# Delta-rule layer: last value product and diagonal transposes moved up, key squares in one instruction, value load ahead of the output load

## What is computed

```python
x = x + _L0_attn_ref(_layernorm(x), ...)        # softmax attention
x = x + _L0_ffn_ref(_layernorm(x), ...)         # 48 experts
x = x + _L1_attn_ref(_layernorm(x), ...)        # the delta rule, below
x = x + _L1_ffn_ref(_layernorm(x), ...)         # 16 experts

# _L1_attn_ref, per head, chunks of 64 tokens
qkv = silu(_causal_conv1d(qkv, conv_weight))    # 4 taps
q, k = _l2norm(q) * Dk ** -0.5, _l2norm(k)
attn = -((k_beta @ k.T) * decay_mask), strictly lower; then a row-by-row solve -> (I - attn)^-1
value_corrected, k_cumdecay = attn @ v_beta, attn @ (k_beta * g_exp)
for c in chunks:
    v_prime = v_c - kcd_c @ state
    out = (q_c @ state) * ge_c + intra @ v_prime
    state = state * gel_c + (k_c * kd_c).T @ v_prime
core = _rmsnorm(core * silu(z), norm_weight); out = core @ W_out
```

## Time and profile before

| | us |
|---|---|
| median of 3 runs | 1714.47 (1711.51 to 1717.37) |
| profiled execution | 1714.89 |
| its span | 1713.2 |
| delta rule, first to last start of a body (15 bodies) | 584.9 to 1533.4 |
| a full body, mean of the 13 from 645.5 to 1476.3 | 63.9 |

### The profile page before, as it was taken

How to read it: one execution, slowest core, us unless ns; L and a number is a source line. 1 busy time by engine, 2 the same in 40 slices (tenths; PEclk the granted TensorE clock), 3 DMA queues, 4 the chain that set the end, 5 groups by cost and what they waited for, 6 DMA issues and landing times. The chain is left out here.

```text
span 1713.2 us, 38604 instructions
## 1 busy us (share of the span) xinstructions
PE 1428.9 (83%) x14345; PEld 1025.2 (60%) x14345; DVE 1139.4 (67%) x2334; ACT 856.3 (50%) x2403; POOL 780.6 (46%) x1118
## 2 busy tenths in 40 slices
PE   5888993199555889999999999999999999986665
PEld 2443442166422667767767767767777777775465
DVE  6886127823566778788778777778788878643623
ACT  3334861043043575665665665665665666532122
POOL 5000000277114266456556466556566656553343
PEclk9998996599776999999999999999999999988688
DMA  8100005085813464554555555654555545241783
GB/s 280 66 2 2 2 1 154 7 234 178 254 49 88 107 146 124 147 149 134 139 146 139 128 152 134 139 147 142 133 147 149 137 143 151 76 117 56 223 259 128
DMA packets 249434, 218.72 MB, mean 128 GB/s; under 512 B 88770, under 2 KB 224962, under 8 KB 247200
## 3 DMA queue, kind: packets, MB, share of 16 engines
q1 hardware_dynamic: 234992, 192.41, 41.4%
q0 software_dynamic: 5712, 15.60, 2.8%
q10 hardware_dynamic: 8544, 8.26, 1.5%
HBM read 133.85 MB, written 82.25 MB: 126 GB/s over the span
## 5 line engine op out<-in xcount | busy, mean ns | idle before, releaser
L1544 PE MATMUL d_big<-all_xn_t,all_w 128*128 128x512 f32 x512 | 264.2, 649 | 17.3 <-DVE d_conv L1805 11.4
L1805 DVE SCALAR_TENSOR_TENSOR d_conv<-d_big,all_cw,d_conv 128x1023 f32<-128x1023 f32 (+2 forms) x192 | 245.4, 1278 | 46.4 <-ACT d_conv L2039 43.8
L2277 POOL TENSOR_TENSOR d_y<-d_y,all_xn 128x256 f32<-128x256 f32 x128 | 95.8, 748 | 183.9 <-DVE d_y L1952 153.0
L1544 PEld LDWEIGHTS d_big<-all_xn_t,all_w 128*128 128x128 f32 x512 | 98.2, 207 | 107.8 <-issue 96.7
L2141 ACT COPY d_ys<-d_big 128x128 f32<-128x128 f32 x256 | 60.9, 266 | 198.5 <-PE d_big L1695 139.5
L1733 PE MATMUL d_big<-all_wo,d_yt 128*128 128x256 f32 x512 | 126.5, 393 | 13.6 <-DVE d_yt L1877 13.6
L1666 PE MATMUL d_big<-all_w,all_xn_t 128*128 128x256 f32 x512 | 124.2, 386 | 0.0
L1851 DVE SCALAR_TENSOR_TENSOR d_AI<-d_big,d_b_col,d_decay 128x256 f32<-128x256 f32 x256 | 105.7, 474 | 23.0 <-PE d_big L1557 20.7
L1733 PEld LDWEIGHTS d_big<-all_wo,d_yt 128*128 128x128 f32 x512 | 97.4, 198 | 26.4 <-issue 14.1
L1666 PEld LDWEIGHTS d_big<-all_w,all_xn_t 128*128 128x128 f32 x512 | 93.6, 190 | 18.3 <-issue 7.2
L347 DVE TENSOR_REDUCE a_neg_max<-a_big 128x1 f32<-128x128 f32 (+7 forms) x128 | 90.5, 751 | 13.1 <-PE a_big L276 12.8
(11 more groups left out here) (437 smaller groups left out, 3503.5 us busy)
## 6 DMA issues: line engine op xcount, KB each, us to landing
turned_kq_scratch<-d_turned SPq DMA_DIRECT2D x32, 512.0 KB, 3.9
d_kq_tok<-turned_kq_scratch SPq DMA_DIRECT2D x128, 128.0 KB, 3.1
turned_v_scratch<-d_vs SPq DMA_DIRECT2D x16, 1024.0 KB, 4.1
d_vs<-turned_v_scratch SPq DMA_DIRECT2D x64, 256.0 KB, 5.6
grouped_y_scratch<-d_yx SPq DMA_DIRECT2D x32, 512.0 KB, 3.9
d_yx<-grouped_y_scratch SPq DMA_DIRECT2D x128, 128.0 KB, 3.1
all_w<-in_L_attn_W_qkvz SPq DMA_DIRECT2D x16, 768.0 KB
...
```

The costliest lines, as they stand in the source:

```text
L1544: mm = pe.matmul(big[0][:, c, :], w_sb[par][:, k, n * DK:(n + 1) * DK], xn_t[:, k, c * 512:(c + 1) * 512], start=(k == 0), stop=(k == KD - 1))
L1805: dve.scalar_tensor_tensor(conv[:, sh:T], src[:, 0:T - sh], cw[:, bass.ds(g, 1), COLUMN_OF[j], 3 - sh], conv[:, sh:T], ALU.mult, ALU.add). ...
L2277: pool.tensor_tensor(part, part, zs[:, t, :], ALU.mult).then_inc(s["yg_s"], 1)
```

## The change

1. `iv 7` of the previous group, with its `gather 7`, moves up: on PE from behind `gates 3` to between `l0y 2` and `gates 2`; on DVE from behind tap 1 3 to behind tap 1 1.
2. `l0x` is split into its three transposes; two of them run ahead of tap 1 3, the third behind `l1p`. `kq_turn 1` moves behind these.
3. `ksq` becomes one Square of all keys into the tile `conv`, and a new step `ksum` on DVE (a tensor_reduce over `conv`, ahead of `kb`) sums them. `tap0 2` waits for `ksum`.
4. ACT: `l1p` directly behind `l0y`, then `silu 1`, `gates 3`, `ksq`, `decay`.
5. DVE: `l2p` directly behind `l1y`, products 0 and 1 behind both. PE: products 2 moves from ahead of `l2y` to behind it.
6. SP: `v_in` goes ahead of the previous group's `y_in 0`.

```diff
 SP_ORDER = steps_of("""
-    this solved, v_out; next kq_out 0; prev y_out 0; next kq_in 0; prev y_in 0; this v_in; next kq_out 1, kq_in 1; prev
+    this solved, v_out; next kq_out 0; prev y_out 0; next kq_in 0; this v_in; prev y_in 0; next kq_out 1, kq_in 1; prev
...
-    l0y 2, gates 2, l0y 3, l0y 4, l0y 5, l0y 6, l0y 7, gates 3; prev iv 7; this l1p 0, l1p 1, l1p 2, l1p 3; next proj 2
-    0, proj 2 1; this l1y 0, l1y 1, l1y 2, l1y 3; next products 0; this l2p 0, l2p 1; next products 1, products 2; this
-    l2y 0, l2y 1; next products 3; this y 0, kv 0, iv 0, ks 1; prev out_mm 0 0; this y 1, qs 1, kv 1, iv 1, ks 2, qs 2;
+    l0y 2; prev iv 7; this gates 2, l0y 3, l0y 4, l0y 5, l0y 6, l0y 7, gates 3, l1p 0, l1p 1, l1p 2, l1p 3; next proj 2
+    0, proj 2 1; this l1y 0, l1y 1, l1y 2, l1y 3; next products 0; this l2p 0, l2p 1; next products 1; this l2y 0, l2y 1;
+    next products 2, products 3; this y 0, kv 0, iv 0, ks 1; prev out_mm 0 0; this y 1, qs 1, kv 1, iv 1, ks 2, qs 2;
...
-    this gates 1; prev sq2 4, o1 7; next tap0 1; prev sq2 5; this gates 2, l0y; next silu 1, ksq 0, ksq 1, ksq 2; this
-    l1p; next ksq 3, decay; this gates 3, l1y, l2p; prev sq2 6, sq2 7; this l2y, ys 0; next tap0 2; this ys 1, o1 1;
+    this gates 1; prev sq2 4, o1 7; next tap0 1; prev sq2 5; this gates 2, l0y, l1p; next silu 1; this gates 3; next ksq,
+    decay; this l1y, l2p; prev sq2 6, sq2 7; this l2y, ys 0; next tap0 2; this ys 1, o1 1;
...
+            def ksum(g, par):
+
+                dve.wait_ge(s["ksq_s"], g + 1)
+                dve.tensor_reduce(ss[:, 0, :], conv[:, :].rearrange("p (t n) -> p t n", t=TT), AX.X, ALU.add).then_inc(s["ksum_s"], 1)
...
-            def ksq(g, par, i):
-
-                if i == 0:
-                    act.wait_ge(s["kq_in0"], g * 64 + 64)
-                    if not at(g, 0):
-                        act.wait_ge(s["ek_s"], g)
-                for t in (2 * i, 2 * i + 1):
-                    act.activation(junk[:, :].rearrange("p (q r) -> p q r", r=QB), kq_tok[:, :, t, :], ACT.Square, accum_out=ss[:, 0, t:t + 1]).then_inc(s["sq_s"], 1)
-                    act.wait_ge(s["sq_s"], g * 16 + t + 1)
+            def ksq(g, par):
+
+                act.wait_ge(s["kq_in0"], g * 64 + 64)
+                act.wait_ge(s["silu_s"], g * NJ + 2)
+                act.activation(conv[:, :].rearrange("p (t q r) -> p q t r", q=NQ, r=QB), kq_tok[:, :, 0:TT, :], ACT.Square
+                               ).then_inc(s["ksq_s"], 1)
```

More of the change, by code:

```diff
@@ L1218 @@
     prev state 6; this v_turn 0; prev r 7, gather 5; this v_turn 1; next tap 0 1, tap 0 2, tap 0 3; this qe; next
-    kq_turn 0; prev gather 6; this l0p; next shift, tap 1 1, tap 1 2, tap 1 3; prev gather 7; this l0x; next kq_turn 1;
-    this l1p; prev y_turn 0; next kb; this l1y; next products 0; this l2p; next products 1; this l2y; next products 2;
+    kq_turn 0; prev gather 6; this l0p; next shift, tap 1 1; prev gather 7; next tap 1 2; this l0x 0, l0x 1; next tap 1
+    3; this l1p, l0x 2; next kq_turn 1; prev y_turn 0; next ksum, kb; this l1y, l2p; next products 0, products 1; this l2y; next products 2;
     this state 0, gather 0, r 1; next products 3; this state 1, gather 1; next tap 2 1; this r 2; next tap 2 2; this
@@ L1315, in delta1_phase @@
         names = ("wg_in dt_in a_in ba_mm gate_a gate_v beta_v cum_v clip_v kx_v gx_v ngx_v gam_v cum_rows edge_rows gamma_s col_mm col_a col_v "
-                 "keep_s wide_s masked blank_s eyed made_v const_s rows_in proj_mm tap_s conv_v silu_s kq_x kq_out0 kq_out1 kq_in0 kq_in1 v_x v_out v_in y_x y_out yx_in wo_s sq_s ek_s sv_s bk_s qe_s x_s exp_s edge_s "
+                 "keep_s wide_s masked blank_s eyed made_v const_s rows_in proj_mm tap_s conv_v silu_s kq_x kq_out0 kq_out1 kq_in0 kq_in1 v_x v_out v_in y_x y_out yx_in wo_s sq_s ksq_s ksum_s ek_s sv_s bk_s qe_s x_s exp_s edge_s "
                  "kk_mm ai_s blk_out blk_in sol_v sol_s sol_out y_in vs_s kout_s p0_mm p0_s y0_mm y0_s x0_s p1_mm p1_s "
@@ L1465, in kq_in @@
                 if not at(g, 0):
-                    sp.wait_ge(s["sq_s"], g * 16 - 8 + 8 * a)
+                    if a:
+                        sp.wait_ge(s["sq_s"], g * 8)
+                    else:
+                        sp.wait_ge(s["ksq_s"], g)
                     sp.sem_inc(s["order"], 1)
@@ L1834, in qe_ @@
             def qe_(g, par):
-                dve.wait_ge(s["sq_s"], g * 16 + 16)
+                dve.wait_ge(s["sq_s"], g * 8 + 8)
                 if not at(g, 0) and not at(g, 1):
@@ L1885, in l0p, with l0x @@
                                          ).then_inc(s["p0_s"], 1)
[L1887 to L1893, removed]
+            def l0x(g, par, n):
+                q = (0, 2, 1)[n]
+                own = slice(QB * q, QB * q + QB)
+                half_of = slice(QB * (q % 2), QB * (q % 2) + QB)
+                dve.wait_ge(s["y0_s"], g * 4 + n + 1)
+                dve.transpose(Xc[own, :, half_of], Y[own, :, own]).then_inc(s["x0_s"], 1)
             def l1p(g, par):
@@ L2007, in first @@
                 kq_turn(0, 0, 1)
+                ksum(0, 0)
                 kb(0, 0)
@@ L2022, in first @@
                     tap(0, 0, 3, sh)
-            loop(dve, DVE_ORDER, dict(tap=tap, shift=shift, kb=kb, qe=qe_, products=products, kq_turn=kq_turn, v_turn=v_turn, y_turn=y_turn, l0p=l0p,
+            loop(dve, DVE_ORDER, dict(tap=tap, shift=shift, ksum=ksum, kb=kb, qe=qe_, products=products, kq_turn=kq_turn, v_turn=v_turn, y_turn=y_turn, l0p=l0p,
                                       l0x=l0x, l1p=l1p, l1y=l1y, l2p=l2p, l2y=l2y, r=residual, state=state, gather=gather,
@@ L2038, in tap0 @@
                     act.wait_ge(s["silu_s"], g * NJ + j)
+                if j == 2:
+                    act.wait_ge(s["ksum_s"], g + 1)
                 act.activation(conv[:, :], big[0][:, :, :].rearrange("p c n -> p (c n)"), ACT.Copy,
@@ L2071, in qsq @@
                                    accum_out=ss[:, 1, t:t + 1]).then_inc(s["sq_s"], 1)
[L2072 removed]
+                    act.wait_ge(s["sq_s"], g * 8 + t + 1)
             def decay(g, par):
@@ L2174, in first @@
                 keep_column(C_EDGE, 2)
-                for i in range(4):
-                    ksq(0, 0, i)
                 silu(0, 0, 1)
+                ksq(0, 0)
                 keep_column(C_OUT, 3)
```

3 lines of the change are left out of this document (1 added, 2 removed).

## The result

| | before | after |
|---|---|---|
| median, us | 1714.72 (1711.51 to 1717.37) | 1826.18 (1824.30 to 1828.54) |
| ratio, 95% interval | | 1.0626 [1.0574, 1.0678] |
| span of the profiled execution | 1713.2 | 1826.7 |
| granted clock, mean over the span | 0.915 | 0.867 |
| mean of the 13 full bodies | 63.9 | 71.6 |

The changed kernel is 6.3% slower by this ratio, which is estimated over the single executions; the quotient of the two medians is 1.0650. The forecast was 1768 us, 3.1% slower. Of the 113.5 us between the spans, 13 x (71.6 - 63.9) = 100 are in the full bodies, 7.4 in the first body (68.1 after, 60.7 before), nothing in the last (57.1 in both). Of the rest, 5.4 are in the start of the delta rule, 590.3 instead of 584.9.

What follows compares the result with a forecast made beforehand. Bodies were taken as bound by PE's work, waits and clock. Per body 2.2 later plus 1.5 clock, times 13, is 48; edge terms, minus 2 for replaced dips, make 53: 1714.9 + 53 = 1768 us, range 1745 to 1790.

Steps and rivals of the forecast that it cites:

- Parts 1, 2: PE before l1p: the 1.90 us wait for DVE's l0x transposes goes, gaining 1.8 us per body; the clock dip behind goes in most.
- Part 3: Key squares: ACT drops eight Squares for one of 1.06 us; DVE gains a reduce of 1.21 us on its way to l2p.
- Part 4: ACT's new order: Exp ends near 1145.9, before DVE scales products 0; the moved 1.28 us table load fits idle time, costing nothing.
- Part 6 and DVE's chain: SP queue and DVE: y_in 0 lands behind v_in, y_turn 0 waits until 1146.45, l2p starts 1150.65; PE waits 5.7 us there.
- Part 5, "Enough; at worst 0.3": PE from l2p to l2y: products 1, about 1 us, covers DVE's copy of 0.7; a loss of 0.3 us at worst.
- The clock, "I take 1.5, the common one": Clock dip behind PE's wait before l2p: costs between 0 and 3.0 us per body, taken as 1.5.
- The small terms: Outside the full bodies: first body 4 us, last 1.5, the reduce in the start-up 1.2 once.
- Rival C: PE's clock stays low from the wait before l2p through y 0, losing over 3.0 us per body: above 1790; chance 0.05.
- Rival A: SP queue: y_in lands by 1142, not held up by v_in, so DVE goes on: 1685 us, 1705 with dips; chance 0.14.

Runs made afterwards that it cites:

- b_prod2: The kernel before with only products 2 moved behind l2y on PE: 1748.44 us, ratio 1.0015 to the kernel before, which took 1747.59 on that chip.
- a_prod2: The changed kernel with products 2 ahead of l2y again on PE: 1790.35 us, ratio 1.0416 to the kernel before.
- a_yturn_late: The changed kernel with y_turn 0 behind the l1y and l2p copies on DVE: 1793.63 us, ratio 1.0261 to the kernel before (1747.59 on that chip).

## Why the prediction was right in direction and too small

Step by step, in the forecast's order:

- **Parts 1, 2.** Right. The wait before l1p is 0.26 (under 0.4 was forecast) and the dip behind it is gone.
- **Part 3.** ksum takes 1.18; 1.21 was taken.
- **Part 4.** Right as to the cost. The Exp ends at 1141.2, long before products 0 are scaled.
- **Part 6 and DVE's chain.** Right. y_turn 0 starts 53.1 us into the body (53.65 forecast), l2p at 57.2 (57.85), vs 2.3 us earlier (about 2). The wait before l2p is 3.8 on the mean and not 5.7, since PE itself arrives later, in six bodies after a pause inside l1y; l2p starts where it was forecast all the same.
- **Part 5, "Enough; at worst 0.3".** Wrong. As work the move costs nothing, as b_prod2 shows; but it puts l2y behind only four of the larger matmuls after a wait of 2.1 to 5.5 us, and a_prod2 shows 36 us for it. The step asked whether DVE's copy is covered, and not what the clock would do in a thinner stretch of PE work.
- **The clock, "I take 1.5, the common one".** This is the term that failed. It was taken from dips behind waits of 1.9, and its upper bound of 3.0 from a body with products 2 still ahead of l2y. Measured: from l2p to the next body 1159.6 - 1145.4 = 14.2 instead of 8.2, so 6.0. The difference of 4.5, less 0.7 by which l2p came earlier than forecast, is 3.8 of the 71.4 - 67.6 in this body, and over all 13 it is 13 x (71.6 - 67.6) = 52 of the 60.5 us that the profiled execution (1828.54) lies above 1768.
- **The small terms.** The first body costs 7.4, not 4, the last 0, not 1.5; the start of the delta rule 5.4, not 1.2, which is scatter.

Rival C, the clock that stays down through y 0, is what happened, and had 0.05. Its own condition was in the text ("PE idles 5.7 us per body"), and the row of the body of 68.0 us already showed l2p at 3.67, behind a pause of 2.68 us inside l1y. The next rows of PE in that body would have said what ends it:

```profile
1468.69 3.38 PE L1557 MATMUL d_big<-d_kq 128*128 128x256 f32 x8
1472.00 2.08 PE L1651 MATMUL d_big<-d_Y,d_edge_p 64*64 64x64 f32 x32
```

Eight matmuls of 128x256 stand between l2p and l2y there, and l2y is at full speed. The change leaves four. Rival A was refuted: y_in came in behind v_in, as the queue's order says. The one thing that a_yturn_late brought up and that no part of the forecast weighed is what an earlier vs does on POOL: the forecast said that v_in's gain is worth nothing, while it is worth less than nothing once kb runs beside it.
